# Relation of block 0 computed chunk by chunk of the depth in four open PSUM banks

## The reference

```
fused    = concat([x, mean_over_tokens(x), cond, cond])        # 4 x 1024 x 1536
relation = relu(fused @ W + b)                                  # 4 x 1024 x 512
h        = relu(quant_linear(relation, w1, b1))                 # 2048 features
out      = x + quant_linear(h, w2, b2)
quant_linear(v, w, b):
    s_in = max(v) / 255;  vq = clip(round(v / s_in), 0, 255) * s_in    # one scale for the whole tensor
    s_w  = max(|w|, per row) / 127;  wq = clip(round(w / s_w)) * s_w
    return vq @ wq.T + round(b / (s_in * s_w)) * (s_in * s_w)
```

## Time and profile before

| | us |
|---|---|
| median of 3 runs (348.91 to 349.14) | 349.14 |
| the profiled execution: its time | 349.02 |
| the profiled execution: span of the trace | 347.2 |
| PE busy | 339.0 (98%) |
| DVE busy | 270.5 (78%) |
| ACT busy | 154.6 (45%) |

### The profile page before, as it was taken

One profiled execution on the slowest core, in us unless ns is written; L12 is line 12 of the kernel. 1 busy time (PEld: TensorE's weight loads), 2 busy tenths in 40 slices (PEclk: granted clock), 3 DMA queues, 4 the chain that ended last, 5 costly groups with the idle time before them and its releaser, 6 DMA issues.

```text
span 347.2 us, 5340 instructions
## 1 busy us (share of the span) xinstructions
PE 339.0 (98%) x1627; PEld 197.3 (57%) x1650; DVE 270.5 (78%) x588; ACT 154.6 (45%) x261; POOL 1.1 (0%) x8
## 2 busy tenths in 40 slices
PE   6999999999999999999999999999999999999995
PEld 5788888888868544444444444444444444444444
DVE  1867668658684679999999999987487595695995
ACT  2625225415412499960000000029959659569700
POOL 1000000000000000000000000000000000000000
PEclk9999999999999999999999999999999999999999
DMA  7966998975432028887781030037984499876206
GB/s 259 397 212 166 337 326 232 279 193 194 98 60 51 12 112 356 347 340 295 315 336 76 0 121 0 0 121 273 418 355 168 142 423 422 343 242 238 95 31 244
DMA packets 29935, 74.92 MB, mean 216 GB/s; under 512 B 17864, under 2 KB 18144, under 8 KB 22496
## 3 DMA queue, kind: packets, MB, share of 16 engines
q1 hardware_dynamic: 29920, 74.73, 59.5%
HBM read 45.37 MB, written 25.17 MB: 203 GB/s over the span
## 4 chain that ended last, share of the span: by engine, by line
PE 92%; issue 3%; DVE 3%; DMA 1%; ACT 0%; DVEq 0%
PE bank L476 28%; PE bank L441 26%; PE bank L358 25%; PE bank L497 4%; PE bank L346 4%; PE bank L451 2%; PE bank L339 1%; DMA x_in<-in_x_dram 1%; DVE hidden L769 1%; PE bank L367 1%; DVE x_lo L609 1%; PE bank L397 1%; PE bank L431 0%; DVE cw_lo L647 0%; PE bank L407 0%
## 5 line engine op out<-in xcount | busy, mean ns | idle before, releaser
L569 ACT ACTIVATE steps<-hidden,s_quant 128x512 int16 (+1 forms) x124 | 76.8, 708 | 98.7 <-DVE s_quant L792 78.1
L441 PE MATMUL bank<-pool_r,w_t 128*128 (+1 forms) x469 | 103.2, 379 | 0.6
L769 DVE TENSOR_SCALAR_CACHE_REDUCE hidden<-bank,qb,hmax 128x512 f32 x128 | 97.6, 809 | 6.2 <-PE bank L451 2.3
L441 PEld LDWEIGHTS bank<-pool_r,w_t 128*128 128x128 bf16 x480 | 47.0, 98 | 56.6
L476 PE MATMUL bank<-w_t 128*128 128x512 bf16 x251 | 55.6, 379 | 0.3
L358 PE MATMUL bank<-x_hi,cw_hi 128*128 128x512 f32 x128 | 51.0, 398 | 0.2 <-DVE x_lo L609 0.2
L358 PE MATMUL bank<-x_lo,cw_hi 128*128 128x512 f32 x128 | 49.9, 390 | 0.0
L358 PE MATMUL bank<-x_hi,cw_lo 128*128 128x512 f32 x128 | 49.9, 390 | 0.0
L614 DVE TENSOR_SCALAR_CACHE_REDUCE hidden<-bank 128x512 f32 (+1 forms) x32 | 22.1, 689 | 29.2 <-PE bank L358 29.2
L476 PEld LDWEIGHTS bank<-w_t 128*128 128x128 bf16 x256 | 25.1, 98 | 30.2 <-issue 0.2
L476 PE MATMUL bank<-w_t,pool_q 128*128 128x512 bf16 x188 | 41.7, 379 | 0.2
(11 more groups left out here) (100 smaller groups left out, 228.7 us busy)
## 6 DMA issues: line engine op xcount, KB each, us to landing
hidden_spill<-hidden SPq DMA_DIRECT2D x16, 1024.0 KB, 3.9
hidden<-hidden_spill SPq DMA_DIRECT2D x16, 1024.0 KB, 8.2
pool_q<-in_L_ffn_w_dram SPq DMA_DIRECT2D x8, 1024.0 KB, 5.5
pool_r<-in_x_dram SPq DMA_DIRECT2D x8, 1024.0 KB, 5.6
x_in<-in_x_dram SPq DMA_DIRECT2D x7, 1024.0 KB, 5.3
out_dram<-pool_r SPq DMA_DIRECT2D x7, 1024.0 KB, 4.1
pool_r<-in_L_cond_W_dram SPq DMA_DIRECT2D x1, 2048.0 KB, 11.0
x_in<-in_x_dram SPq DMA_DIRECT2D x2, 512.0 KB, 5.2
```

The source lines that it names most:

```text
L441: mm = pe.matmul(bank[ft % BANKS][:, :], w1_t[:, ft, k, :], act_q[:, bass.ds(n * (KD * TB) + k * TB, TB)], start=(k == 0), stop=(k == KD - 1))
L569: ins = act.activation(steps[:, q % 2, f, :], hidden[:, bass.ds(slot * HB + ft * TB, TB)], ACT.Copy, scale=s_quant[:, ft:ft + 1])
L769: dve.tensor_scalar(hidden[:, bass.ds(slot * HB + ft * TB, TB)], bank[ft % BANKS][:, :], qb1[:, ft:ft + 1], hmax[:, ft:ft + 1], ALU.add, A ...
```

## The change

Three things are rewritten.

1. Loads. Block 0's x comes in four transfers, one for each chunk of the depth (128 partitions x 4 pieces of 128 elements, 512 bytes a piece), instead of two halves of its tokens (one run of 4 KB in a partition). The four loads of the weight W go from SP's queue to ACT's, ahead of ACT's first activation. The three small loads of rows stand on SP's queue behind the four of x.
2. PE in block 0. The loop over chunks is outermost: all four output quarters are open at once in banks 4 to 7. Between the products of a chunk PE turns the next chunk. The rows of biases are turned in bank 3, behind the first chunk's eight products. The last chunk closes the banks one after the other, and block 1 is turned behind the first closing.
3. DVE. The cast of the bias columns stands behind chunk 0. For block 0, DVE takes the four banks with one `x_lo` of block 1 behind each; after them `scale_w(0)` and `cast_w(0)` stand next to each other. Blocks 1 to 3 are written out and no longer in a loop; their order is that of `phase1_block` as before.

```diff
-            load_half(0, x0_landed)
-            load_cw(range(KD // 2))
-            load_half(1, x_landed[0])
+            x_first = x_blocks[0].rearrange("p (j d) -> p j d", d=D)
+            for k in range(KD):
+                sp.dma_start(x_in[:, 0, :, k * P:(k + 1) * P], x_first[:, :, k * P:(k + 1) * P]
+                             ).then_inc(x0_landed[k], 16)
             sp.dma_start(cond_rows, cond.rearrange("b (k p) -> b k p", p=P)).then_inc(rows_landed, 16)
             sp.dma_start(condb_rows, cond_b.rearrange("(k p) -> k p", p=P)).then_inc(rows_landed, 16)
             sp.dma_start(b1_rows, b1.rearrange("(k p) -> k p", p=P)).then_inc(rows_landed, 16)
-            load_cw(range(KD // 2, KD))
             load_x(1, 1)
...
-            for h, landed in enumerate((x0_landed, x_landed[0])):
-                keep_warm((20, 9)[h], ident_bf[:, :], REL[0])
-                pe.wait_ge(landed, 16)
...
+            REL0 = bank[4:8]
+            def turn_x0(k):
+                pe.wait_ge(x0_landed[k], 16)
+                for j in range(TJ):
+                    mm = pe.transpose(XT[k][:, j * P:(j + 1) * P], x_in[:, 0, j, k * P:(k + 1) * P], ident[:, :])
+                mm.then_inc(x_turned, 1)
+            def product0(k, ot, w, v):
+                return pe.matmul(REL0[ot][:, :], w[:, k, ot * P:(ot + 1) * P], v[:, 0, k, :],
+                                 start=(k == 0 and w is cw_hi and v is x_hi),
+                                 stop=(k == KD - 1 and w is cw_lo))
...
+            keep_warm(30, ident_bf[:, :], bank[4])
+            turn_x0(0)
+            keep_warm(6, ident_bf[:, :], bank[5])
+            for k in range(KD - 1):
+                pe.wait_ge(cw_hi_ready, k + 1)
+                pe.wait_ge(hi_ready, k + 1)
+                for ot in range(KD):
+                    product0(k, ot, cw_hi, x_hi)
+                pe.wait_ge(cw_lo_ready, k + 1)
+                for ot in range(KD):
+                    product0(k, ot, cw_lo, x_hi)
+                if k == 0:
+                    turn_columns()
+                if k + 1 == KD - 1:
+                    pe.wait_ge(cols_taken, 1)
+                turn_x0(k + 1)
+                pe.wait_ge(lo_ready, k + 1)
+                for ot in range(KD):
+                    product0(k, ot, cw_hi, x_lo)
...
+            for ot in range(KD):
+                product0(k, ot, cw_hi, x_lo)
+                product0(k, ot, cw_lo, x_hi).then_inc(rel_done, 1)
+                if ot == 0:
+                    turn_x(1, 1, 1)
...
-            for k in range(KD // 2):
-                take_cw(k)
-            take_hi(0, 0, range(KD // 2))
-            for k in range(KD // 2, KD):
+            for k in range(KD):
+                act.dma_start(cw_in[:, k, :], cw_rows[:, k, :]).then_inc(cw_landed[k], 16)
+            for k in range(KD):
                 take_cw(k)
                 take_hi(0, 0, [k])
...
-            with dve.Fori(0, KD // 2) as it:
-                for par in range(2):
-                    phase1_block(2 * it + par, it, par, False, False)
+            for ot in range(KD):
+                take_relation(0, ot, bank[4 + ot])
+                take_lo(1, 1, [ot])
+            scale_w(0, 0, 0, False)
+            cast_w(0)
+            for n in range(1, KD):
+                phase1_block(n, n // 2, n % 2, False, False)
```

More of the change, by code:

```diff
@@ L138, in adaln_quantized_ffn @@
         REL = bank[4:6]
-        x0_landed = sem("x0_landed")
+        x0_landed = [sem(f"x0_landed{k}") for k in range(KD)]
         x_landed = [sem("x_landed0"), sem("x_landed1")]
@@ L213, in load_w @@
                 sp.dma_start(dst, src).then_inc(w_landed[par], 16)
-            def load_half(h, landed):
-                half = slice(h * TJ // 2, (h + 1) * TJ // 2)
-                sp.dma_start(x_in[:, 0, half, :].rearrange("p j d -> p (j d)"),
-                             x_blocks[0, :, half.start * D:half.stop * D]).then_inc(landed, 16)
-            def load_cw(chunks):
-                for k in chunks:
-                    sp.dma_start(cw_in[:, k, :], cw_rows[:, k, :]).then_inc(cw_landed[k], 16)
-            load_half(0, x0_landed)
-            load_cw(range(KD // 2))
-            load_half(1, x_landed[0])
+            x_first = x_blocks[0].rearrange("p (j d) -> p j d", d=D)
+            for k in range(KD):
+                sp.dma_start(x_in[:, 0, :, k * P:(k + 1) * P], x_first[:, :, k * P:(k + 1) * P]
+                             ).then_inc(x0_landed[k], 16)
             sp.dma_start(cond_rows, cond.rearrange("b (k p) -> b k p", p=P)).then_inc(rows_landed, 16)
@@ L372, in _ @@
-            pe.wait_ge(rows_landed, 48)
-            turned = bank[7]
-            for k in range(CK):
-                pe.transpose(turned[:, k * B:(k + 1) * B], cond_rows[:, k, :], ident[0:B, 0:B])
-            pe.transpose(turned[:, CONDB_AT:CONDB_AT + KD], condb_rows, ident[0:KD, 0:KD])
-            pe.transpose(turned[:, B1_AT:B1_AT + FT], b1_rows, ident[0:FT, 0:FT]).then_inc(cols_turned, 1)
+            REL0 = bank[4:8]
[4 more added lines that the diff above has]
+                mm.then_inc(x_turned, 1)
@@ new lines, in product0, with turn_columns @@
+            def product0(k, ot, w, v):
+                return pe.matmul(REL0[ot][:, :], w[:, k, ot * P:(ot + 1) * P], v[:, 0, k, :],
+                                 start=(k == 0 and w is cw_hi and v is x_hi),
+                                 stop=(k == KD - 1 and w is cw_lo))
+            def turn_columns():
+                pe.wait_ge(rows_landed, 48)
+                turned = bank[3]
+                for k in range(CK):
+                    pe.transpose(turned[:, k * B:(k + 1) * B], cond_rows[:, k, :], ident[0:B, 0:B])
+                pe.transpose(turned[:, CONDB_AT:CONDB_AT + KD], condb_rows, ident[0:KD, 0:KD])
+                pe.transpose(turned[:, B1_AT:B1_AT + FT], b1_rows, ident[0:FT, 0:FT]).then_inc(cols_turned, 1)
@@ L378, in _ @@
+            k = KD - 1
+            pe.wait_ge(cw_hi_ready, KD)
+            pe.wait_ge(hi_ready, KD)
+            for ot in range(KD):
+                product0(k, ot, cw_hi, x_hi)
+            pe.wait_ge(lo_ready, KD)
+            pe.wait_ge(cw_lo_ready, KD)
+            for ot in range(KD):
[3 more added lines that the diff above has]
+                    turn_x(1, 1, 1)
             with pe.Fori(0, NB // 2 - 1) as it:
-                for par in range(2):
-                    n = 2 * it + par
+                for par in (1, 0):
+                    n = 2 * it + 2 - par
@@ L381, in _ @@
                     relation(n, par, 0)
-                    turn_x(n + 1, it + par, 1 - par)
+                    turn_x(n + 1, it + 2 - par, 1 - par)
                     for ot in range(1, KD):
                         relation(n, par, ot)
-            n = NB - 2
-            relation(n, 0, 0)
-            turn_x(n + 1, NB // 2 - 1, 1)
-            for ot in range(1, KD):
-                relation(n, 0, ot)
             pe.wait_ge(mean_ready, 2)
```

43 lines of the change are left out of this document (19 added, 24 removed).

## The result

The changed kernel takes 355.76 us (median of 4 runs, 355.61 to 356.53); the kernel before, run beside it, 349.02 (4 runs, 348.70 to 349.14). The ratio is 1.0197, 95% interval 1.0184 to 1.0210: slower by 6.7 us. 354.1 was predicted, with a range of 352.0 to 357.2.

A forecast was written before the change was run, and what follows sets the result against it. PE was taken to bound phase 1 (busy 75.95 of 75.95 us). Head -0.75 plus three waits +5.65 gave +4.9, so 353.9 to 354.0; uncosted late risks made it 354.1, range 352.0 to 357.2.

The forecast's parts named there:

- E: Moment PE ends block 0's products: 23.3 us against 24.05 before, a gain of 0.75.
- The rows' wait: PE in block 0, after chunk 0's products: waits for the bias rows, taken to land at 10.4 us.
- the rest of the head: PE from the rows' landing to the end of block 0's products: 12.65 us plus some 0.25 for handovers.
- the head gains nothing: Start of the kernel, by the skill's queue rule: x and W come no sooner; time 0.75 us above the sum.
- The three waits of block 1: PE waits for DVE's takes ahead of the first, third and fourth relations: 1.3, 1.85 and 2.45 us, together 5.65.
- DVE's stop: DVE stands idle ahead of the first cast until ACT has quantized, about 2.6 us.
- The first cast: DVE's cast of W1's chunk 0, behind scale_w(0): ends near 33 us instead of 23.5.
- x of block 4: load_x(4) on SP's queue: issued near 51, landing 56.3, needed at 57; covered by 0.7; loss taken 0, up to 1.5.
- Nothing is given back: After block 1, PE is the bound without a gap, so block 2 and all later blocks stay 4.9 us late.
- the likeliest one: The forecast's own case, the summed terms holding: 353 to 355.6 us, chance 0.66.
- B: Rival, worse than the sum: x late or slow, load_x(4) late, or PE's clock falling in waits; 356 to 359, chance 0.16.
- C: Rival, faster than before: block 1's takes come early enough to hide DVE's stop; 348.4 us or less, chance 0.05.

The follow-up runs named there:

- relaxed condition: Changed kernel, block 1's first two relations on PE waiting only for the bank they write (1 and 2 takes, not 3 and 4): 356.56 us, ratio 1.0207.
- the best version: Changed kernel with scale_w(0) early, ACT's rounding reordered, rows one chunk later, relaxed condition, block 1's x_lo early, 2 MB load cut in four: 347.64 us, ratio 0.9949.
- all edits but the split load: Changed kernel with scale_w(0) early, ACT's cw_hi early, rows one chunk later, relaxed condition, block 1's x_lo ahead of takes 2 to 4: 349.45 us, ratio 1.0014.

## Why the prediction was right, and where its sum was short

- *E, the end of block 0's products*: 23.3 predicted, 23.20 measured. The rows' wait was where it was put, with its end at 9.94 instead of 10.4. That the sum is closer than its parts is luck: 12.9 was said for the rest of the head (12.65 and 0.25 for handovers), and it took 13.26. Moving the rows by a chunk showed that this wait sets it. The rule of the Trainium skill that was weighed here ("DMA: Bandwidth & Descriptors", Issuing engines are not separate DMA queues) is not contradicted: 220 GB/s in the first 7 us with two queues, 222 with one. The conclusion drawn from it, that the head gains nothing, did not come true (0.85 gained): less has to land before the first product, which started at 7.01 instead of 10.53.
- *The three waits of block 1*: 1.3, 1.85 and 2.45 predicted, 1.25, 1.61 and 2.19 measured, plus 0.42 of restarts that were not in the sum: 5.47 against 5.65. The cause of the two long ones is shown from both sides, by taking it out of the changed kernel and by putting it into the one before. The first stays when `scale_w(0)` is early (1.07 idle), so it belongs to the four takes behind the closing banks. The relaxed condition showed that the three are one chain of DVE, whose end the sum had nearly right. DVE's stop was 2.63 where about 2.6 was said. The first cast ended at 32.74 where 33 was said.
- *x of block 4*: this is the term that was mis-sized. "I take 0", up to 1.5; it was 1.91. I had carried over the distance of 12.0 from `load_w(3)` to `load_x(4)` as if it were a constant. Of the 12.0, 8.95 were the transpose's time on the queue, which depends on what else has been queued: `load_x(3)` stood 6.6 us ahead of `load_w(3)` before (26.61 and 33.23) and 1.5 after (37.15 and 38.65), so both and the 2 MB of W's rows were in the queue together; the transpose took 11.28 and b2 2.12, and the distance became 14.45. The load in four parts brought the transpose to 7.94 and took the wait away. The slack of 0.7 us that was found was smaller than the 2.45 by which the distance grew, and that is why 0 was the wrong value to take.
- *Nothing is given back*: so it was; 6.54 late at 52.06/58.60 and 6.62 at the end of phase 1.
- The sum of the terms was 4.9, the measured 6.5. The time, 355.76, lies between two cases: 0.2 above the likeliest one (353 to 355.6, chance 0.66) and 0.2 below B (356 to 359), whose late `load_x(4)` came true while its two other parts did not show in the profiled execution. The stated range held because it had room for B. C (DVE's stop not felt) was off by what was said: the waits that it would have had to save were 1.61 and 2.19. Versions in which the stop is really gone ended at 350.7 with the first wait left, and at 347.64 with that one, the rows' wait and the late x gone too.

## What to carry to other kernels

When a change gathers work that was interleaved, look in each engine's instruction order for a pair whose second member waits for another engine: what lay between them was the cover, and everything behind the second member inherits the wait. Then follow the late signal into the DMA queue: a distance between two issues read from a trace holds only for the same queue contents (here it grew by 2.45 us), so a slack below a microsecond is not cover. And remove such waits from the last one backwards, since an earlier one taken out alone only moves into the later. Last, test the parts of a change one by one: here the loads alone may bring half of what the best version gains, without any of the prices.

## What the runs showed of the hardware

**TensorE's clock falls in some executions behind a wait of about 2 us.** The prediction had a fall as part of rival B, at 2.7 us. The kernel with `load_x(4)` ahead of the transpose had one in its profile: PE waited 2.12 us for the rows, and in the next two microseconds the granted clock was 0.50, the level of 1.2 GHz. TensorE in order of time, then busy time by stretch (length, PE, PEld, DVE, ACT, POOL, granted clock, DMA share, GB/s):

```profile
10.56 0.28 PE L374 MATMUL bank<-ident,pool_r 4*128 4x4 f32 x2 [2.12 <-DMA pool_r<-in_L_ffn_b_dram]
...
26.45 0.51 PE L352 MATMUL bank<-x_hi,cw_hi 128*128 128x512 f32 x1 [1.07 <-DVE hidden L640]
```

```profile
10.00:12.00 2.00, 1.44 (x10) 1.32 (x11) 0.74 (x5) 0.40 (x1) 0.00 (x0) 0.87 0.96 384
12.00:14.00 2.00, 2.00 (x6) 1.51 (x6) 1.78 (x3) 0.81 (x3) 0.00 (x0) 0.50 1.05 389
14.00:16.00 2.00, 2.00 (x10) 1.58 (x9) 0.00 (x0) 0.00 (x0) 0.00 (x0) 0.78 1.05 389
```

Block 1 starts at 26.45 instead of 24.45: the rows were 0.6 later than in the kernel after, and the rest is the clock. The same followed the wait of 1.82 for the rows in the kernel with the relaxed condition (0.50 between 12 and 14 us), the wait of 2.00 with the loads alone (0.57 between 10 and 14 us), the wait of 2.05 in the kernel before with DVE's order, and the one of 2.03 in the kernel with the rows later (for the last two, the stretches that hold the fall):

```profile
35.00:40.00 5.00, 2.95 (x8) 2.14 (x8) 4.56 (x9) 2.43 (x4) 0.00 (x0) 0.75 1.02 271
```

```profile
36.00:42.00 6.00, 4.36 (x12) 3.47 (x13) 3.93 (x8) 1.80 (x3) 0.00 (x0) 0.72 0.99 296
```

These five are all the traces with a fall, one in each. Other waits as long left the clock at 1.00: a second one of 2.04 in the kernel with `load_x(4)` ahead, one of 2.01 in the kernel with the relaxed condition, 2.03 in the kernel after, 2.00 in the one with the split load. So the same wait can end either way from run to run. It can be counted by a run's mean granted clock, low being 0.995 or less:

| kernel | longest wait of PE in its trace, from 2 us on | runs with a low mean clock |
|---|---|---|
| before (beside the experiments) | 1.07 | 0 of 57 |
| fastest version | 0.23 | 0 of 6 |
| loads alone, 32 keep-warm matmuls | 0.99 | 1 of 12 |
| `scale_w(0)` early | 1.07 | 2 of 6 |
| the same with ACT's order | 1.57 | 3 of 12 |
| all edits but the split load | 1.66 | 1 of 12 |
| after | 2.03 | 1 of 4 |
| loads alone | 2.00 | 5 of 12 |
| `load_x(4)` ahead; relaxed condition; split load | 2.12; 2.01; 2.00 | 3 of 6; 3 of 5; 3 of 5 |
| DVE's order in the kernel before; rows later | 2.05; 2.03 | 2 of 5; 2 of 5 |

Low clocks are more frequent where the trace has a wait of 2 us, but they do occur in kernels whose trace shows none; those runs have no trace, so what PE did in them is not known. The theory behind the 32 keep-warm matmuls, that no execution would fall, failed by one run, and 1 against 5 of 12 is too few to call the matmuls the cause.

With the loads alone the seven other runs took 347.88 to 348.57 and those five 349.87 to 350.47: one fall costs about 2 us there. Where PE would soon have waited for x anyway, it cost little: with DVE's order in the kernel before the two runs with a fall took 354.24 and 354.43, the three without 353.54 to 354.50. The Trainium skill ("TensorE: Matmul & The Clock Gate", Part 1) says that idleness brings the lower level back, and these traces agree in so far as each fall stands behind a wait of 1.82 to 2.12 us. The falls may be part of why some edits, the split load above all, showed more gain in the trace than in the median.

**A DMA transpose's time on its queue is not its own**: the first, third and fourth of w1's transposes took 2.0 to 5.4 us in all traces; the second, behind the 2 MB load, took 8.95 before, 11.28 after, 12.39 with one more load of x ahead of it, and 7.94 with the 2 MB load cut in four.

**Loading x in pieces of 512 bytes** cost more on the queue, 2.77 us for four issues (0.69 each, against 0.40 and 0.43 for the two halves of the same block before), and in the kernel after a chunk of 256 KB landed 6.2 us after its issue (median of four), where a half of 512 KB took 5.2 before.
